# The first expert layer written without a loop over batches: weights loaded in order of need, two buffers of x, and the transposes, routing and normalisation of one batch placed inside its neighbours

## The chip, the cores and the metric

The kernel runs on one core of one Trainium2 chip. A core has a matmul engine (TensorE, PE in the rows, whose weight loads are listed apart as PEld), a vector engine (DVE), an activation engine (ACT), a general engine (GpSimd, POOL) and a synchronising engine (SP) that here only issues transfers; a row marked SPq or POOLq is a transfer being issued. The metric is the device time of one execution in microseconds; lower is better.

## The reference

Four layers run in sequence on x of shape (4, 512, 256): windowed attention, a mixture of experts, a gated delta rule, and a second mixture of experts, each followed by a residual sum and a layer norm. The change touches only the second of them:

```
B, S, D = x.shape                       # 4, 512, 256; E = 8 experts, K = 2
logits = xf @ gate_w
top_logits, top_idx = jax.lax.top_k(logits, K)
top_gates = jax.nn.softmax(top_logits, axis=-1)
gates = jnp.sum(jax.nn.one_hot(top_idx, E) * top_gates[..., None], axis=1)
h = gelu(jnp.einsum('nd,edh->neh', xf, w1) + b1)          # 256 -> 128 for each expert
out_e = jnp.einsum('neh,ehd->ned', h, w2) + b2            # 128 -> 256
routed = jnp.einsum('ne,ned->nd', gates, out_e)
shared = gelu(xf @ shared_w1 + shared_b1) @ shared_w2 + shared_b2   # 256 -> 256 -> 256
x = _layernorm(x + routed + shared)
```

All eight experts are computed for every token, and the gates weigh their outputs.

## The kernel before

The layers are functions that run one after the other, with a barrier of all engines between them; x passes from one to the next through a tensor in HBM (`mid_x` in the rows; each function reads one and writes another). `layer0_experts` (names with `f_`) works on a batch of 512 tokens at a time, four in all. It has ten hidden units of 128: units 0 and 1 are the shared expert, units 2 to 9 the eight experts.

On TensorE a batch goes through these steps. The tokens x are transposed, eight blocks of 128x128 (L705), into two PSUM banks `turn0` and `turn1`, and ACT copies them to `xT` (L752). Sixteen matmuls of 8 columns each make the routing logits (L710; a float32 matmul is two rows of the trace, a transpose one). `hide(n)` makes hidden unit n: four rows of 512 columns into one of two banks `hid` (L718), which ACT turns into `h` through gelu (L761), one of four buffers. The gates, made by DVE from the logits (L792 to L809, with one Exp on ACT, L754), are transposed in four rows (L738) and copied by ACT (L758). `project(u)` makes a sum: u = 0 is the shared expert's two units plus the biases weighted by the gates (16 rows of L728 and 8 of L731), every other u one expert (8 rows of L728), into one of two banks `sum`. DVE adds each sum into y, weighted by its gate (L815 for u = 0, with x; L818 for the others), then measures mean and variance (L823, L827, L829), POOL raises the variance to the power -0.5 (L772), DVE normalises (L833) and POOL issues the store (L775).

The order on each engine is the order of the code, and semaphores tie the engines: `hide(n)` waits for the gelu of unit n-2, `project(u)` for the gelu of its own unit and for the sum of u-2 to have been added. TensorE's order within a batch is hide 0, 1, 2, transpose of the gates, then hide(3+u) and project(u) in turns, which leaves project 7 and 8 (and, after hide 9, project 6) without a hide between them.

Every engine runs its part in a hardware loop over the four batches (`Fori`), and the whole of a batch is done before the next begins. At the start SP issues twelve loads (identity, gate weights, b2, w2, w1, b1) on one semaphore `loaded`, for which TensorE, ACT and DVE all wait in full, and then x of batch 0. There is one buffer of x: x of the next batch is issued when the last sum of the batch before has been added (`sp.wait_ge(added, F_SUMS * b)`, L694).

Of the kernel before, what the change touches and what calls it, by code (L numbers as in the profile page):

```python
# [18 lines left out]
ALU = mybir.AluOpType  # L19
# [615 lines left out]
def layer0_experts(nc, d):  # L635

    ctx, sems = ExitStack(), []
    with ctx:
# [14 lines left out]
        x, xT = sb("x", [P, NT, C]), sb("xT", [P, CK, T])  # L653
# [14 lines left out]
        loaded, x_in, x_turned, xT_ready, consts = sem("loaded"), sem("x_in"), sem("x_turned"), sem("xT_ready"), sem("consts")  # L668
# [5 lines left out]
        k_chain = 10  # L674

        carrier, carrier_pool = sem("carrier"), sem("carrier_pool")
        block = ctx.enter_context(nc.Block())

        @block.sync
        def _(sp):  # L680
            loads = [(ident[:], d["c_ident"]), (w_gate[:], d["L0_ffn_gate_w"].rearrange("(k p) n -> p k n", p=P)),
                     (b2[0:F_E, :], d["L0_ffn_b2"]), (b2[F_E:F_E + 1, :], d["L0_ffn_shared_b2"].rearrange("(a n) -> a n", a=1)),
                     (w2[:, 0:F_SH, :], d["L0_ffn_shared_w2"].rearrange("(k p) n -> p k n", p=P)),
                     (w2[:, F_SH:, :], d["L0_ffn_w2"].rearrange("e p n -> p e n"))]
            for k in range(CK):
                loads += [(w1[:, k, 0:F_SH, :], d["L0_ffn_shared_w1"][k * P:(k + 1) * P, :].rearrange("p (e n) -> p e n", e=F_SH)),
                          (w1[:, k, F_SH:, :], d["L0_ffn_w1"][:, k * P:(k + 1) * P, :].rearrange("e p n -> p e n"))]
            for dst, src in loads:
                sp.dma_start(dst, src).then_inc(loaded, 16)
            with nc.allow_non_contiguous_dma(reason="biases, one value a partition"):  # L690
                sp.dma_start(b1[:, 0:F_SH], d["L0_ffn_shared_b1"].rearrange("(e p) -> p e", p=P)).then_inc(loaded, 16)
                sp.dma_start(b1[:, F_SH:], d["L0_ffn_b1"].rearrange("e p -> p e")).then_inc(loaded, 16)
            with sp.Fori(0, BATCH) as b:
                sp.wait_ge(added, F_SUMS * b)  # L694
                sp.dma_start(x[:], x1_b[b, :, :, :]).then_inc(x_in, 16)

        @block.tensor
        def _(pe):
            pe.wait_ge(loaded, 16 * 12)
            with pe.Fori(0, BATCH) as b:  # L700
                pe.wait_ge(x_in, 16 * b + 16)
                pe.wait_ge(gT_ready, b)
                for k in range(CK):
                    for t in range(NT):
                        last = nc.tensor.transpose(TB[k][:, t * P:(t + 1) * P], x[:, t, k * P:(k + 1) * P], ident[:])  # L705
                last.then_inc(x_turned, 1)
                pe.wait_ge(xT_ready, 2 * b + 2)
                for t in range(NT):
                    for k in range(CK):
                        last = nc.tensor.matmul(TB[0][:, t * F_E:(t + 1) * F_E], xT[:, k, t * P:(t + 1) * P], w_gate[:, k, :],  # L710
                                                start=k == 0, stop=k == CK - 1)
                last.then_inc(routed, 1)

                def hide(n):

                    pe.wait_ge(gelued, F_UNITS * b + max(n - 1, 0))
                    for k in range(CK):
                        last = nc.tensor.matmul(HB[n % 2][:], w1[:, k, n, :], xT[:, k, :], start=k == 0, stop=k == CK - 1)  # L718
                    last.then_inc(hidden, 1)

                def project(u):

                    chunks = range(F_SH) if u == 0 else [u + F_SH - 1]
                    pe.wait_ge(gelued, F_UNITS * b + chunks[-1] + 1)
                    pe.wait_ge(added, F_SUMS * b + max(u - 1, 0))
                    for t in range(NT):
                        for n in chunks:
                            last = nc.tensor.matmul(YB[u % 2][:, t, :], h[:, n % 4, t * P:(t + 1) * P], w2[:, n, :],  # L728
                                                    start=n == chunks[0], stop=u > 0)
                        if u == 0:  # L730
                            last = nc.tensor.matmul(YB[0][:, t, :], gatesT[:, t * P:(t + 1) * P], b2[:], start=False, stop=True)  # L731
                    last.then_inc(summed, 1)

                for n in range(F_SH + 1):
                    hide(n)
                pe.wait_ge(gated, b + 1)
                for t in range(NT):
                    last = nc.tensor.transpose(TB[1][0:F_E + 1, t * P:(t + 1) * P], gates[:, t, :], ident[:])  # L738
                last.then_inc(g_turned, 1)
                pe.wait_ge(gT_ready, b + 1)  # L740
                for u in range(F_SUMS):
                    if F_SH + 1 + u < F_UNITS:
                        hide(F_SH + 1 + u)
                    project(u)

        @block.scalar
        def _(act):
            act.wait_ge(loaded, 16 * 12)
            with act.Fori(0, BATCH) as b:
                act.wait_ge(x_turned, b + 1)  # L750
                for k in range(CK):
                    nc.scalar.activation(xT[:, k, :], TB[k][:], ACT.Copy).then_inc(xT_ready, 1)  # L752
                act.wait_ge(shifted, b + 1)
                nc.scalar.activation(weight[:], weight[:], ACT.Exp).then_inc(exped, 1)  # L754
                for n in range(F_UNITS):
                    if n == F_SH + 1:
                        act.wait_ge(g_turned, b + 1)
                        nc.scalar.activation(gatesT[:], TB[1][0:F_E + 1, :], ACT.Copy).then_inc(gT_ready, 1)  # L758
                    act.wait_ge(hidden, F_UNITS * b + n + 1)
                    act.wait_ge(summed, F_SUMS * b + (0 if n < 4 else max(n - 4 - F_SH + 2, 1)))  # L760
                    nc.scalar.activation(h[:, n % 4, :], HB[n % 2][:], ACT.Gelu, bias=b1[:, n:n + 1]).then_inc(gelued, 1)  # L761

        @block.gpsimd
        def _(pool):
# [5 lines left out]
            with pool.Fori(0, BATCH) as b:  # L770
# [8 lines left out]
        def _(dve):  # L779
            dve.wait_ge(loaded, 16 * 12)  # L780
            dve.wait_ge(consts, 4)
            with dve.Fori(0, BATCH) as b:
                count = [0]

                def link(ins):

                    count[0] += 1
                    ins.then_inc(chain, 1)
                    dve.wait_ge(chain, k_chain * b + count[0])

                dve.wait_ge(routed, b + 1)
# [12 lines left out]
                link(nc.vector.tensor_tensor(mask[:], swapped[:, :, 0:F_E], logits[:, :, 0:F_E], ALU.not_equal))  # L804
                dve.wait_ge(exped, b + 1)
# [3 lines left out]
                nc.vector.tensor_tensor(gates[:, :, 0:F_E], weight[:], total[:, :, None].broadcast_to([P, NT, F_E]),  # L809
                                        ALU.mult).then_inc(gated, 1)  # L810
                dve.wait_ge(gated, b + 1)
                for u in range(F_SUMS):
# [1549 lines left out]
```

## Time and profile before

| | |
|---|---|
| time before, median of 3 runs | 2175.42 us |
| the three runs | 2175.3, 2175.42, 2187.16 us |
| the profiled execution: its own time | 2183.15 us |
| the profiled execution: its span (first to last instruction) | 2181.5 us |
| mean granted TensorE clock of the span | 0.878 |
| busy share PE / PEld / DVE / ACT / POOL | 78% / 50% / 48% / 30% / 32% |
| the stretch of `layer0_experts`, first load issued to last store issued | 599.93 to 833.73 us |

The profiled execution took 1.65 us more than its span and 7.7 us more than the median of the three runs. Of its 2181.5 us, the changed function has 234, or 11%. A clock of 1.00 in the rows is TensorE at 2.4 GHz, 0.50 at 1.2 GHz.

### The profile page before, as it was taken

What the parts mean: (1) busy time and instruction counts of PE and PEld (TensorE: products, weight loads), DVE (VectorE), ACT (ScalarE), POOL (GpSimd) and SP (SyncE); (2) the same over time, 40 slices, a digit from 0 to 9 for tenths busy, and PEclk for the clock granted to TensorE, in tenths of its full rate; (3) what the DMA queues carried; (4) which work ended last, traced back from release to release, by engine and by line L of the source; (5) the groups of instructions that cost most, each with busy time, mean ns of one, the idle gap of its engine ahead of it and who ended that gap; (6) DMA issues with size and microseconds to landing.
All of it is one profiled execution on the core that took longest, in us unless ns stands there. A gap on an engine that the chain in (4) does not pass through costs nothing. (4 is left out here: it accounts for less than half of the span.)

```text
span 2181.5 us, 29241 instructions
## 1 busy us (share of the span) xinstructions
PE 1692.8 (78%) x10666; PEld 1080.1 (50%) x10666; DVE 1050.4 (48%) x2394; ACT 659.2 (30%) x1159; POOL 692.0 (32%) x1099
## 2 busy tenths in 40 slices
PE   4887887988668885546699999999999964677771
PEld 3443444444345553222366666666666753444651
DVE  4746355462213332354556666776676521333623
ACT  2141431513212222323344444444544310111010
POOL 2010200200000000002767777787777631000142
PEclk8999898999879887867899999999999865888596
DMA  1000000000020002224112222212222213110074
GB/s 44 1 1 1 20 1 20 1 1 11 11 60 19 19 19 65 77 83 99 25 35 40 49 50 49 40 33 46 39 41 44 35 25 86 63 63 29 22 164 107
DMA packets 215799, 89.29 MB, mean 41 GB/s; under 512 B 166441, under 2 KB 208658, under 8 KB 215426
## 3 DMA queue, kind: packets, MB, share of 16 engines
q1 hardware_dynamic: 202658, 66.99, 13.9%
q0 software_dynamic: 6960, 18.88, 3.2%
q10 hardware_dynamic: 6064, 1.86, 0.4%
q8 instruction: 74, 1.21, 0.2%
q14 instruction: 43, 0.35, 0.1%
HBM read 53.39 MB, written 34.31 MB: 40 GB/s over the span
## 5 line engine op out<-in xcount | busy, mean ns | idle before, releaser
L1641 DVE SCALAR_TENSOR_TENSOR d_conv<-d_prep,d_cw,d_conv 128x511 f32<-128x511 f32 (+2 forms) x288 | 214.5, 746 | 39.7 <-ACT d_conv L1470 32.9
L1256 PE MATMUL d_prep<-d_hT,d_w 128*128 128x512 f32 x384 | 189.9, 619 | 27.1 <-DMA d_cw<-L_attn_conv_wq 18.3
L1592 POOL TENSOR_TENSOR d_prod<-d_blk 64x30 f32<-64x30 f32 (+4 forms) x360 | 174.3, 484 | 102.8 <-DMA d_blk<-mid_a_blk 75.6
L1596 POOL TENSOR_TENSOR d_blk<-d_blk,d_prod 64x30 f32<-64x30 f32 (+4 forms) x360 | 184.9, 514 | 28.2
L419 ACT ACTIVATE a_probs<-a_acc 128x896 f32<-128x896 f32 x128 | 117.5, 918 | 220.4 <-PE a_acc L244 132.0
L516 DVE TENSOR_REDUCE a_top<-a_turn 128x4 f32<-128x512 f32 (+3 forms) x240 | 147.3, 652 | 62.0 <-PE a_turn L207 54.0
L465 POOL TENSOR_TENSOR a_rstd<-a_rstd,a_mhalf 128x4 f32<-128x4 f32 x4 | 4.1, 1028 | 407.7 <-DVE a_rstd L565 407.7
L1256 PEld LDWEIGHTS d_prep<-d_hT,d_w 128*128 128x128 f32 x384 | 68.5, 198 | 88.4 <-issue 69.4
L1295 PE MATMUL d_prep<-d_kq 128*128 128x256 f32 x384 | 96.6, 396 | 15.3 <-DVE d_qkT L1673 15.3
L1470 ACT ACTIVATE d_conv<-d_prep,d_cw 128x512 f32<-128x512 f32 x96 | 66.1, 689 | 139.7 <-PE d_prep L1256 139.5
L1295 PEld LDWEIGHTS d_prep<-d_kq 128*128 128x128 f32 x384 | 73.6, 199 | 43.8 <-DVE d_qkT L1673 27.1
L206 PE MATMUL a_turn<-a_kS,a_qS 128*128 128x128 bf16 (+3 forms) x256 | 64.9, 306 | 32.6 <-DVE a_top L516 29.5
L718 PE MATMUL f_hid<-f_xT,f_w 128*128 128x512 f32 x160 | 82.6, 646 | 5.2 <-ACT f_gatesT L758 3.5
L728 PE MATMUL f_sum<-f_w,f_h 128*128 128x256 f32 x320 | 77.9, 384 | 0.1
L818 DVE SCALAR_TENSOR_TENSOR f_y<-f_sum,f_gates,f_y 128x256 f32<-128x256 f32 x128 | 53.1, 477 | 47.1 <-PE f_sum L728 46.6
L1583 POOL TENSOR_TENSOR d_mean<-d_mean,d_mhalf 128x16 f32<-128x16 f32 x12 | 38.9, 3241 | 108.5 <-DVE d_mean L1753 108.5
L772 POOL TENSOR_TENSOR f_rstd<-f_rstd,f_mhalf 128x4 f32<-128x4 f32 x4 | 4.1, 1030 | 217.9 <-DVE f_rstd L829 217.9
L451 POOL TENSOR_SCALAR a_stack<-a_parts 128x64 bf16<-128x64 bf16 x128 | 33.8, 297 | 120.6 <-DVE a_parts L501 120.6
L728 PEld LDWEIGHTS f_sum<-f_w,f_h 128*128 128x128 f32 x320 | 59.5, 190 | 25.1 <-issue 17.4
L1671 DVE SCALAR_TENSOR_TENSOR d_AT<-d_prep,d_a,d_decay 128x128 f32<-128x128 f32 x192 | 58.2, 346 | 22.3 <-PE d_prep L1295 21.9
L1445 ACT ACTIVATE d_kq<-d_conv 128x512 f32<-128x512 f32 x96 | 60.4, 629 | 24.4 <-DVE d_conv L1641 22.2
L1515 ACT ACTIVATE d_decay<-d_dec 128x512 f32<-128x512 f32 x48 | 28.7, 598 | 122.6 <-PE d_dec L1284 122.5
(353 smaller groups left out, 3728.7 us busy)
## 6 DMA issues: line engine op xcount, KB each, us to landing
mid_gate<-p_gate POOLq DMA_DIRECT2D x4, 768.0 KB, 4.0
mid_v<-p_v_tok POOLq DMA_DIRECT2D x3, 1024.0 KB, 6.0
d_v_h<-mid_v SPq DMA_DIRECT2D x12, 256.0 KB, 5.8
d_gate_h<-mid_gate SPq DMA_DIRECT2D x12, 256.0 KB, 5.5
mid_a_blk<-d_AT SPq DMA_DIRECT2D x48, 64.0 KB, 2.0
d_blk<-mid_a_blk SPq DMA_DIRECT2D x12, 256.0 KB, 3.6
mid_u_blk<-d_blk SPq DMA_DIRECT2D x12, 256.0 KB, 2.9
mid_l_blk<-d_blkT SPq DMA_DIRECT2D x12, 256.0 KB, 3.7
```

What stands on the lines that cost most here:

```text
L206: nc.tensor.matmul(acc, q[:, i * P:(i + 1) * P], k[:, 0:w], start=True, stop=False)
L419: nc.scalar.activation(probs[:, g % 2, h % 4, u, 0:896], AB[u][:].rearrange("p a t -> p (a t)")[:, 0:896], ACT.Exp, scale=A_SCALE).then_in ...
L516: nc.vector.tensor_reduce(dst, src, AX.X, ALU.max).then_inc(maxed, 1)
L718: last = nc.tensor.matmul(HB[n % 2][:], w1[:, k, n, :], xT[:, k, :], start=k == 0, stop=k == CK - 1)
L728: last = nc.tensor.matmul(YB[u % 2][:, t, :], h[:, n % 4, t * P:(t + 1) * P], w2[:, n, :], start=n == chunks[0], stop=u > 0)
L1256: last = nc.tensor.matmul(PB[f % 2][:], w[:, n % 2, i, k, :], hT[:, k, b * T:(b + 1) * T], start=k == 0, stop=k == CK - 1)
L1295: last = nc.tensor.matmul(PB[f % 2][:, 2 * c * P:2 * (c + 1) * P], kq[:, n % KQ_BUFS, 0, b, t0:t0 + P], kq[:, n % KQ_BUFS, :, b, t0:t0 + P ...
L1445: nc.scalar.activation(kq[:, n % KQ_BUFS, i, b, :], conv[:, f % 2, :], ACT.Silu).then_inc(silued, 1)
L1470: nc.scalar.activation(conv[:, f % 2, :], PB[f % 2][:], ACT.Copy, scale=cw[:, n % 2, f % 2, TAPS - 1:TAPS]).then_inc(scaled, 1)
L1592: nc.gpsimd.tensor_tensor(pr, blk[:, 0:t, t:t + 1].broadcast_to([lanes, t, m]), blk[:, t:t + 1, t + 1:BLK].broadcast_to([lanes, t, m]), AL ...
L1596: nc.gpsimd.tensor_tensor(blk[:, 0:t, t + 1:BLK], blk[:, 0:t, t + 1:BLK], pr, ALU.subtract).then_inc(subst, 1)
L1641: ins = nc.vector.scalar_tensor_tensor(dst, PB[f % 2][:, 0:T - j], cw[:, n % 2, f % 2, TAPS - 1 - j:TAPS - j], dst, ALU.mult, ALU.add)
```

## The change

The loops over batches become plain Python loops, so that each engine has the instructions of all four batches in a row and pieces of one batch can stand between those of another.

- Loads: identity, x of batch 0 and the gate weights come first; TensorE and ACT wait for identity and gate weights (`first_in`) and for x. Then the six transfers of w1 and b1 (`w1_in`, waited for before the first hide and, on ACT, before the first gelu), then b2 and w2 (`w2_in`, before the first project), then x of batch 1. x of batch 2 and 3 is issued when the first sum of batch b-2 has been added.
- Two buffers of x, xT, gates and y, by the parity of the batch.
- TensorE: batch b+1 is transposed after project 2 of batch b, routed after project 3, its gates transposed after project 7; hides 0 and 1 of batch b+1 take the place between project 6, 7 and 8 where batch b has no hide left.
- ACT: the copies of xT stand after gelu 5, the Exp after gelu 8, the copy of the gates after gelu 0 of the next batch.
- DVE: the routing of batch b+1 stands after the sums 3 (`choose`) and 5 (`weigh`), the normalisation of batch b-1 after sum 1 of batch b.

```diff
-        x, xT = sb("x", [P, NT, C]), sb("xT", [P, CK, T])
+        x, xT = sb("x", [P, 2, NT, C]), sb("xT", [P, 2, CK, T])
-        gates, gatesT = sb("gates", [P, NT, F_E + 1]), sb("gatesT", [F_E + 1, T])
+        gates, gatesT = sb("gates", [P, 2, NT, F_E + 1]), sb("gatesT", [F_E + 1, T])
-        y, x2 = sb("y", [P, NT, C]), sb("x2", [P, NT, C])
+        y, x2 = sb("y", [P, 2, NT, C]), sb("x2", [P, NT, C])
...
         @block.sync
...
-            for dst, src in loads:
-                sp.dma_start(dst, src).then_inc(loaded, 16)
...
-            with sp.Fori(0, BATCH) as b:
-                sp.wait_ge(added, F_SUMS * b)
-                sp.dma_start(x[:], x1_b[b, :, :, :]).then_inc(x_in, 16)
+            def load_x(b):
+                if b >= 2:
+                    sp.wait_ge(added, F_SUMS * (b - 2) + 1)
+                    sp.sem_inc(carrier_sp)
+                sp.dma_start(x[:, b % 2, :, :], x1_b[b, :, :, :]).then_inc(x_in[b % 2], 16)
+
+            sp.dma_start(ident[:], d["c_ident"]).then_inc(first_in, 16)
+            load_x(0)
...
+            for b in range(1, BATCH):
+                load_x(b)
...
         @block.tensor
-            pe.wait_ge(loaded, 16 * 12)
-            with pe.Fori(0, BATCH) as b:
+            pe.wait_ge(first_in, 32)
...
+            def hide(b, n):
+                unit = F_UNITS * b + n
+                if unit == 0:
+                    pe.wait_ge(w1_in, 16 * 6)
+                if unit >= 2:
+                    pe.wait_ge(gelued, unit - 1)
...
+            def project(b, u):
+                chunks = range(F_SH) if u == 0 else [u + F_SH - 1]
+                total_u = F_SUMS * b + u
+                if total_u == 0:
+                    pe.wait_ge(w2_in, 16 * 4)
+                if u == 0:
+                    pe.wait_ge(gT_ready, b + 1)
+                pe.wait_ge(gelued, F_UNITS * b + chunks[-1] + 1)
+                if total_u >= 2:
+                    pe.wait_ge(added, total_u - 1)
...
+            turn_x(0)
+            route(0)
+            hide(0, 0)
+            hide(0, 1)
+            for b in range(BATCH):
+                hide(b, F_SH)
+                if b == 0:
+                    turn_gates(0)
                 for u in range(F_SUMS):
                     if F_SH + 1 + u < F_UNITS:
-                        hide(F_SH + 1 + u)
-                    project(u)
+                        hide(b, F_SH + 1 + u)
+                    elif b + 1 < BATCH:
+                        hide(b + 1, F_SH + 1 + u - F_UNITS)
+                    project(b, u)
+                    if b + 1 < BATCH:
+                        if u == 2:
+                            turn_x(b + 1)
+                        if u == 3:
+                            route(b + 1)
+                        if u == 7:
+                            turn_gates(b + 1)
...
         @block.scalar
...
+            keep_x(0)
+            raise_gates(0)
+            act.wait_ge(w1_in, 16 * 6)
+            for b in range(BATCH):
                 for n in range(F_UNITS):
...
+                    if n == (1 if b else F_SH + 1):
+                        keep_gates(b)
+                    gelu(b, n)
+                    if b + 1 < BATCH:
+                        if n == 5:
+                            keep_x(b + 1)
+                        if n == 8:
+                            raise_gates(b + 1)
...
         @block.vector
...
+            choose(0)
+            weigh(0)
+            for b in range(BATCH):
+                for u in range(F_SUMS):
+                    add(b, u)
+                    if u == 1 and b:
+                        normalise(b - 1)
+                    if b + 1 < BATCH:
+                        if u == 3:
+                            choose(b + 1)
+                        if u == 5:
+                            weigh(b + 1)
+                measure(b)
+            normalise(BATCH - 1)
```

On TensorE, the end of one batch and the start of the next stand like this before: the last hide (`f_hid`, 512 columns) and the projects 6 to 8 (`f_sum`) close the loop's body,

```order
 L718 MATMUL f_hid<-f_xT,f_w 128x512 x2
 L725 REGISTER_ALU
 L728 MATMUL f_sum<-f_w,f_h 128x256 x4
 L724 REGISTER_ALU
 L725 REGISTER_ALU
 L728 MATMUL f_sum<-f_w,f_h 128x256 x4
 L724 REGISTER_ALU
 L725 REGISTER_ALU
 L728 MATMUL f_sum<-f_w,f_h 128x256 x4
 L700 REGISTER_ALU
 L700 COMPARE_AND_BRANCH
```

and the body begins again with the transposes of x (`f_turn` from `f_x`), the routing (`f_turn` from `f_xT`) and hides 0 and 1:

```order
 L700 ISA
 L705 MATMUL f_turn<-f_ident,f_x 128x128 x8
 L707 ISA
 L710 MATMUL f_turn<-f_w_gate,f_xT 128x8 x8
 L716 REGISTER_ALU
 L718 MATMUL f_hid<-f_xT,f_w 128x512 x4
```

In the changed kernel, on the same engine in the middle of batch 0 (hide 5, project 2 and on):

```order
 L741 MATMUL f_hid<-f_xT,f_w 128x512 x2
 L756 MATMUL f_sum<-f_w,f_h 128x256 x4
 L717 MATMUL f_turn<-f_ident,f_x 128x128 x8
 L741 MATMUL f_hid<-f_xT,f_w 128x512 x2
 L756 MATMUL f_sum<-f_w,f_h 128x256 x4
 L724 MATMUL f_turn<-f_w_gate,f_xT 128x8 x8
 L741 MATMUL f_hid<-f_xT,f_w 128x512 x2
 L756 MATMUL f_sum<-f_w,f_h 128x256 x4
```

The transposes and the routing of batch 1 have moved between hides and projects of batch 0. On ACT the piece around them is this now (gelus are `f_h`, the Exp of the routing `f_weight`):

```order
 L791 ACTIVATE f_xT<-f_turn 128x512 x2
 L806 ACTIVATE f_h<-f_hid,f_b 128x512 x3
 L795 ACT_TABLE_LOAD
 L795 ACTIVATE f_weight<-f_weight 128x32
 L806 ACT_TABLE_LOAD
 L806 ACTIVATE f_h<-f_hid,f_b 128x512 x2
 L799 ACTIVATE f_gatesT<-f_turn 9x512
```

where before both table loads stood ahead of a batch's first gelu:

```order
 L752 ACT_TABLE_LOAD
 L752 ACTIVATE f_xT<-f_turn 128x512 x2
 L754 ACTIVATE f_weight<-f_weight 128x32
 L759 ISA
 L760 REGISTER_ALU
 L761 ACT_TABLE_LOAD
 L761 ACTIVATE f_h<-f_hid,f_b 128x512
```

The pair of table loads has moved from the head of a batch to between gelu 8 and gelu 9 of the batch before. SP's queue is now, with x of batch 0 (L688) second where it stood thirteenth:

```order
 L690 DMA f_ident<-c_ident 128x128
 L688 DMA f_x<-mid_x 128x4x256
 L692 DMA f_w_gate<-L_ffn_gate_w 128x2x8
 L694 DMA f_w<-L_ffn_shared_w 128x256 x2
 L696 DMA f_b<-L_ffn_shared_b 128x2x1
 L697 DMA f_b<-L_ffn_b 128x8x1
 L699 DMA f_w<-L_ffn_w 128x8x128 x2
 L703 DMA f_b<-L_ffn_b 8x256
 L703 DMA f_b<-L_ffn_shared_b 1x256
 L703 DMA f_w<-L_ffn_shared_w 128x2x256
 L703 DMA f_w<-L_ffn_w 128x8x256
 L688 DMA f_x<-mid_x 128x4x256 x3
```

All of w1 and b1 stand ahead of b2 and w2, and x of batch 1 follows the weights without waiting for anything.

## Rows read from the trace of the kernel before

**Rows 1.** Stretch: length, busy PE PEld DVE ACT POOL, clock, DMA share, GB/s

```profile
668.74:722.99 54.25, 46.17 (x157) 29.30 (x157) 20.04 (x67) 11.14 (x16) 1.83 (x2) 0.88 0.06 19
```

**Rows 2.** Timeline at the stage's start: start, length, instruction [idle before, releaser]

```profile
600.33 0.43 SPq L689 DMA_DIRECT2D f_w_gate<-L_ffn_gate_w  x1
...
609.54 1.46 SPq L695 DMA_DIRECT2D f_x<-mid_x  x1
613.11 1.28 ACT L752 ACT_TABLE_LOAD   x1 [30.20 <-DMA f_b<-L_ffn_b]
...
614.34 1.97 PE L705 MATMUL f_turn<-f_ident,f_x 128*128 128x128 f32 x8 [26.01 <-DMA f_x<-mid_x]
```

**Rows 3.** Timeline from the last matmuls of batch 0 to batch 1's fourth hide

```profile
657.29 5.64 PE L728 MATMUL f_sum<-f_w,f_h 128*128 128x256 f32 x24
664.79 0.39 SPq L695 DMA_DIRECT2D f_x<-mid_x  x1
668.74 1.97 PE L705 MATMUL f_turn<-f_ident,f_x 128*128 128x128 f32 x8 [5.81 <-DMA f_x<-mid_x]
671.89 3.58 PE L710 MATMUL f_turn<-f_w_gate,f_xT 128*128 128x8 f32 x16 [1.18 <-ACT f_xT L752]
675.32 5.24 PE L718 MATMUL f_hid<-f_xT,f_w 128*128 128x512 f32 x8
682.81 0.60 PE L738 MATMUL f_turn<-f_ident,f_gates 128*9 128x128 f32 x4
684.30 1.98 PE L718 MATMUL f_hid<-f_xT,f_w 128*128 128x512 f32 x4 [0.89 <-ACT f_gatesT L758]
```

**Rows 4.** Timeline in the middle of batch 0, one hide and project

```profile
645.24 1.88 PE L718 MATMUL f_hid<-f_xT,f_w 128*128 128x512 f32 x4
646.96 1.89 PE L728 MATMUL f_sum<-f_w,f_h 128*128 128x256 f32 x8
647.24 0.69 ACT L761 ACTIVATE f_h<-f_hid,f_b 128x512 f32<-128x512 f32 x1 [2.83 <-PE f_hid L718]
648.68 1.88 PE L718 MATMUL f_hid<-f_xT,f_w 128*128 128x512 f32 x4
648.89 1.66 DVE L818 SCALAR_TENSOR_TENSOR f_y<-f_sum,f_gates,f_y 128x256 f32<-128x256 f32 x4 [1.78 <-PE f_sum L728]
```

**Rows 5.** Timeline, start of project 0 of batch 0 and the hide behind it

```profile
631.61 1.03 PE L728 MATMUL f_sum<-f_w,f_h 128*128 128x256 f32 x4
...
638.25 1.98 PE L718 MATMUL f_hid<-f_xT,f_w 128*128 128x512 f32 x4
```

**Rows 6.** Timeline, the transposes of batch 2

```profile
722.99 1.97 PE L705 MATMUL f_turn<-f_ident,f_x 128*128 128x128 f32 x8 [5.56 <-DMA f_x<-mid_x]
```

**Rows 7.** Transposes, matmuls of the next function: timeline

```profile
843.05 30.38 SPq L921 DMA_DIRECT2D p_x<-mid_x  x4
848.34 1.97 PE L943 MATMUL p_turn<-p_ident,p_x 128*128 128x128 f32 x8 [21.85 <-DMA p_x<-mid_x]
859.32 1.04 PE L943 MATMUL p_turn<-p_ident,p_x 128*128 128x128 f32 x8
```

**Rows 8.** Transfers in 604 to 606 us and 610 to 612 us

```profile
DMA packets 649, 0.66 MB, mean 332 GB/s; under 512 B 1, under 2 KB 649, under 8 KB 649
DMA packets 2031, 0.41 MB, mean 206 GB/s; under 512 B 1276, under 2 KB 2031, under 8 KB 2031
```

**Rows 9.** Timeline, the Exp of batch 0

```profile
622.28 0.23 ACT L754 ACTIVATE f_weight<-f_weight 128x32 f32<-128x32 f32 x1 [4.85 <-DVE f_weight L798]
```

**Rows 10.** Stretches as in rows 1: this stage, delta rule early, delta rule late

```profile
627.00:640.00 13.00, 12.11 (x40) 6.25 (x39) 1.23 (x1) 1.86 (x4) 0.00 (x0) 1.00 0.00 0
1200.00:1300.00 100.00, 94.45 (x659) 67.28 (x658) 66.52 (x147) 47.02 (x91) 70.55 (x104) 1.00 0.32 54
1740.00:1760.00 20.00, 18.45 (x106) 14.63 (x105) 6.03 (x17) 1.39 (x5) 17.57 (x32) 0.50 0.00 0
```

**Rows 11.** Timeline, one run of narrow matmuls in the last of these stretches

```profile
1749.16 1.92 PE L1394 MATMUL d_rec<-d_S,d_kq 128*128 128x32 f32 x8
```

More of the change, by code:

```diff
@@ L709, in _ @@
                     for k in range(CK):
-                        last = nc.tensor.matmul(TB[0][:, t * F_E:(t + 1) * F_E], xT[:, k, t * P:(t + 1) * P], w_gate[:, k, :],
+                        last = nc.tensor.matmul(TB[0][:, t * F_E:(t + 1) * F_E], xT[:, b % 2, k, t * P:(t + 1) * P], w_gate[:, k, :],
                                                 start=k == 0, stop=k == CK - 1)
                 last.then_inc(routed, 1)
[L714 to L732, printed above, removed]
@@ L734, in _, with turn_gates @@
-                for n in range(F_SH + 1):
-                    hide(n)
+            def turn_gates(b):
                 pe.wait_ge(gated, b + 1)
                 for t in range(NT):
-                    last = nc.tensor.transpose(TB[1][0:F_E + 1, t * P:(t + 1) * P], gates[:, t, :], ident[:])
+                    last = nc.tensor.transpose(TB[1][0:F_E + 1, t * P:(t + 1) * P], gates[:, b % 2, t, :], ident[:])
                 last.then_inc(g_turned, 1)
-                pe.wait_ge(gT_ready, b + 1)
+            def hide(b, n):
[4 more added lines that the diff above has]
+                    pe.wait_ge(gelued, unit - 1)
+                for k in range(CK):
+                    last = nc.tensor.matmul(HB[unit % 2][:], w1[:, k, n, :], xT[:, b % 2, k, :], start=k == 0, stop=k == CK - 1)
+                last.then_inc(hidden, 1)
@@ new lines, in project @@
+            def project(b, u):
[8 more added lines that the diff above has]
+                    pe.wait_ge(added, total_u - 1)
+                for t in range(NT):
+                    for n in chunks:
+                        last = nc.tensor.matmul(YB[total_u % 2][:, t, :], h[:, (F_UNITS * b + n) % 4, t * P:(t + 1) * P], w2[:, n, :],
+                                                start=n == chunks[0], stop=u > 0)
+                    if u == 0:
+                        last = nc.tensor.matmul(YB[total_u % 2][:, t, :], gatesT[:, t * P:(t + 1) * P], b2[:], start=False, stop=True)
+                last.then_inc(summed, 1)
@@ L753, in _, with keep_gates @@
                 act.wait_ge(shifted, b + 1)
                 nc.scalar.activation(weight[:], weight[:], ACT.Exp).then_inc(exped, 1)
-                for n in range(F_UNITS):
[L756 to L761, printed above, removed]
+            def keep_gates(b):
+                act.wait_ge(g_turned, b + 1)
+                nc.scalar.activation(gatesT[:], TB[1][0:F_E + 1, :], ACT.Copy).then_inc(gT_ready, 1)
@@ L779, in _, with link, choose @@
         def _(dve):
-            dve.wait_ge(loaded, 16 * 12)
             dve.wait_ge(consts, 4)
[L782 to L789, printed above, removed]
+            count = [0]
+            def link(ins):
+                count[0] += 1
+                ins.then_inc(chain, 1)
+                dve.wait_ge(chain, count[0])
+            def choose(b):
                 dve.wait_ge(routed, b + 1)
@@ L836, in _ @@
                 dve.wait_ge(ln_done, b + 1)
[L837 removed]
+            choose(0)
+            weigh(0)
+            for b in range(BATCH):
+                for u in range(F_SUMS):
[9 more added lines that the diff above has]
+            normalise(BATCH - 1)
     nc.clear_and_free_semaphores(sems)
```

85 lines of the change are left out of this document (52 added, 33 removed).

## The prediction

> **What bounds the kernel now.** The page's chain of waits doesn't reach back to this function (it names only lines of the last function), so I read the stretch directly: first the busy times of one batch, then the timeline through it, then the two places where TensorE stands still. From the transposes of batch 1 to those of batch 2 are 54.25 us, of which TensorE is busy 46.2, DVE 20.0, ACT 11.1, POOL 1.8 [rows 1, 3, 6]. Only TensorE is near full. In the middle of a batch it has no gap: hide starts follow each other at 645.24 and 648.68, so hide and project take 3.44 us, 1.72 each, while one gelu takes 0.69 and one sum on DVE 1.66 [rows 4]. So the stage is bound by TensorE, and what counts is what a batch takes beyond its matmuls at full clock. Two things are beyond: TensorE waits from 662.93 (657.29 + 5.64) to 668.74 for x, which was only issued at 664.79, and then the transposes, the routing and the first hides run one behind the other with waits between them, at half clock: eight rows of hides take 5.24 us there, where four from start to start take 1.72 in mid-batch [rows 3, 4]. The mean clock of the batch is 0.88 [rows 1]. At the stage's start TensorE waits until 614.34 for x, issued thirteenth at 609.54 [rows 2].
>
> **The boundary between batches.** I work it out in two ways.
>
> First by content. A batch in the changed kernel is, on TensorE: ten hides, 10 x 1.72 = 17.2; projects 1 to 8, 8 x 1.72 = 13.8; project 0, from 631.61 to 638.25, 6.6 [rows 4, 5]; eight transposes; sixteen rows of routing; four of the gates, 0.6 [rows 3]. The transposes took 1.97 at half clock; the same eight of the next function took 1.04 at full clock, with the drain of the last, about 0.9 from start to start [rows 3, 7]. The routing took 3.58 and no row shows it at full clock: it is 1.8 if it halves as the transposes do, 3.6 if it doesn't; I take 1.8, since its spacing (3.58/16 = 0.22) is that of the transposes at half clock (1.97/8 = 0.25, drain included). Sum 17.2 + 13.8 + 6.6 + 0.9 + 1.8 + 0.6 = 40.9, against 54.25: 13.3 less, 11.5 if the routing stays at 3.6.
>
> Then by what goes. The gap for x: 5.8 before batch 1, 5.6 before batch 2 [rows 3, 6]. From the transposes to the fourth hide: 684.30 - 668.74 = 15.6 becomes 0.9 + 1.8 + 3 x 1.72 + 0.6 = 8.5, so 7.1. The last three projects of a batch run without a hide and take 5.64 where 3 x 1.72 = 5.2 would do: 0.4 [rows 3]. Together 13.2. I take 13.3 a boundary. There are three: **40 us**. The order shown of TensorE has nothing else in it: the number of matmuls stays.
>
> What hides the moved work, and what it costs if the cover is gone:
> - x of the next batch. x of batch 1 stands right behind the weights, x of batch 2 and 3 is issued after the first sum of the batch before the one that runs, a whole batch ahead, and takes 3.7 to 4.0 us from issue to the transposes (664.79 to 668.74) [rows 3]. Cost nothing.
> - Copies of xT. ACT makes two, done about 1.2 us after the transposes (idle of 1.18 before the routing [rows 3]), and between transposes and routing now stand a hide and a project, 3.44, with gelu 6 behind the copies. Spare 2 us.
> - The routing on DVE. Logits to gates took from 675.3 to before 682.81, with the Exp in between [rows 3]. Now `choose` has from project 3 to gelu 8 and `weigh` until after project 7: more than two pairs, 7 us, and DVE is at 20 of now 41 us, a sum of 1.66 in every 3.44. Sums wait behind the routing for about 2 us once, but `project(u)` waits only for the sum of u-2. Cost nothing.
> - The two table loads on ACT now stand between gelu 8 and gelu 9. Load, Exp, load, gelu are 1.28 + 0.23 + 1.28 + 0.69 = 3.5 [rows 2, 9, 4]. Behind gelu 9 TensorE's hide 1 of the next batch waits, which starts three pairs and the gates' transposes after hide 8: 3 x 3.44 + 0.6 = 10.9. Gelu 8 is over 2.7 after hide 8 starts (647.24 - 645.24 + 0.69), and the second load comes after hide 9: 3.44 + 2.0 + 1.28 + 0.69 = 7.4. Spare 3.5 us. Cost nothing, and if the Exp came 5 us late, about 1.5 a boundary.
> - Normalisation and store of a batch (POOL 1.0, DVE 1.4) leave the boundary, where they cost nothing either. They remain behind the last batch, with the same tail as before.
>
> **The stage's start.** x goes from the thirteenth place to the second. It is issued at 600.33, in the place of the gate weights [rows 2]. Before, the transposes followed an issue of x by 3.95 (batch 1), 4.8 (batch 0, behind the weights) and 5.3 (next function, behind nine small loads: 843.05 to 848.34) [rows 2, 3, 7]. That is 604.3 to 605.6; I take 604.8, the middle row, for 614.34: 9.5 less. Then hide 0 would come 6.6 later (transposes, copies, routing at half clock as before, 668.74 to 675.32 [rows 3]), at 611.4, and must find w1 and b1. Ahead of them in the queue are identity and x; with the 1.3 MB of w1 that makes 1.9 MB, at 332 GB/s 5.7 us; the 1276 tiny packets of b1 slowed a stretch of 2 us to 206 GB/s, 0.8 us [rows 8]. From a start of the flow at about 603 that gives 609.5, before 611.4. The other end is that they land no earlier than the whole did before, when ACT saw all twelve at 613.11 [rows 2]: 1.7 lost. b2 and w2 are needed only after three hides and the gates, past 618, when all had landed at 613.11 even with x behind. So **9.5 us**, bounds 7.0 (605.6 and 613.1) to 10.0.
>
> **The sum.** 40 + 9.5 = 49.5. The profiled execution would take 2183.15 - 49.5 = 2133.7; it stands 7.7 above the median of the runs, and nothing in its trace says where, so I take the difference off the median: 2175.42 - 49.5 = **2126 us**. The known bounds are 3 x 11.5 + 7.0 = 41.5 and 3 x 13.6 + 10.0 = 51: 2124 to 2134.
>
> **A rule against a row.** The granted clock is 1.00 with TensorE 93% busy in this stage (627 to 640) and 94% busy early in the delta rule, but 0.50 with it busy 18.45 of 20 us in the late delta rule [rows 10], where the rows include eight matmuls of 32 columns at a time [rows 11]. So being busy has not kept the clock up everywhere, and the change puts its narrowest work, the routing of 8 columns, into the middle of full-clock hides. The Trainium skill (TensorE: Matmul & The Clock Gate, "HAM oscillation — how this bites in real kernels") gives as its abstract rule that idle gaps of TensorE are to be avoided. By that rule no clock would be lost here, since no gap is left; by the row a loss can't be excluded, and it is the first rival below.
>
> **Rivals.**
> (1) The narrow block takes the clock down once a batch. Then transposes, routing and gates cost their half-clock time, 3.3 us more, and the hides behind them run as in rows 3 (5.24 for eight where 3.44 would do, 1.8 more): 5.1 a boundary, 15 in all, 2141. For it: rows 10 and 11. Against: the gates' transposes, also narrow, stand inside 627 to 640 at 1.00, and a project and a hide now stand between transposes and routing.
> (2) The overlap is won only in part: a moved step arrives late at each boundary and TensorE, whose order is fixed, stands before it. If the piece at the boundary is as long as today's wait for x (5.7), 17 come back, with w1 late 1.7 more: 2145. For it: three engines now hand over within a running batch (TensorE to ACT to DVE to ACT to DVE to TensorE). Against: the spares of 2 to 7 us above.
> (3) The change doesn't do what it says: x or w1 still come last because the transfers share the engines instead of following the queue. Then the front gives 0 to 3 instead of 9.5, and the boundaries still 40: 2132 to 2136. Against: x was issued last and was last to land.
> (4) Slower than before: denser work is granted half the clock. All four batches at 0.50 are 4 x 2 x 40.9 = 327 us where full clock takes 164; the 163 more outweigh the 49.5 won: 2289. It decides from the point where 30% of the matmul time (49.5/164) runs at half clock. For it: the row at 0.50 with TensorE 92% busy. Against: the same stretch is of narrow matmuls, and with wide ones the delta rule held 1.00 over 100 us at 94% busy [rows 10].
>
> **How the numbers follow.** Forecast (2124 to 2134, with the scatter of runs) 0.65; (1) 0.10; (2) 0.09; (3) 0.08; (4) 0.03; the rest, 0.05, is a mishap not named that eats most of the gain. The three runs lie within 12 us of each other, so a median can stand some us above the sum. The range 2117 to 2143 holds the forecast, (3), most of (1). Within 1% of 2175.42 is within 21.8 us, about what a measurement of this kernel can tell from no change; 2153.7 is its lower edge. Forecast, (1), (2) and (3) all lie below it: faster 0.92. Same 0.05, slower 0.03.
>
> **What would show it.** In the changed kernel's timeline: the first transposes near 604.8, the first hide near 611.4 without a wait for w1; from then on no idle of TensorE over 0.5 us until the last project; batches 41 us apart (from project 0 to project 0); the routing in 1.8 us; granted clock 1.00 from some 10 us after the first matmul on; the last store issued near 784 instead of 833.73. Waits of the routing for f_xT, of the gates' transposes for DVE, or of a hide for gelu 9 would show (2). A clock under 0.95 between 620 and 770 would show (1) or (4). The prediction is wrong if the rest of the program moves: its code is the same, so any shift there above the scatter would be a cause that I have not seen.

## The result

The changed kernel takes 2128.89 us in the median of four runs (2124.86 to 2131.51), the kernel before 2177.81 in the median of four (2175.3 to 2187.16): a ratio of 0.9762, 95% interval 0.9739 to 0.9785. That is 48.9 us less by the medians; 49.5 was predicted, as 2126 us.

The profiled execution of the changed kernel took 2124.86 us. Its timeline at the stage's start (start, length, instruction), to be held against [rows 2]:

```profile
597.52 0.35 SPq L690 DMA_DIRECT2D f_ident<-c_ident  x1
597.92 0.43 SPq L688 DMA_DIRECT2D f_x<-mid_x  x1
...
601.98 1.97 PE L717 MATMUL f_turn<-f_ident,f_x 128*128 128x128 f32 x8 [16.03 <-DMA f_w_gate<-L_ffn_gate_w]
...
605.19 3.58 PE L724 MATMUL f_turn<-f_w_gate,f_xT 128*128 128x8 f32 x16 [1.24 <-ACT f_xT L791]
608.62 5.05 PE L741 MATMUL f_hid<-f_xT,f_w 128*128 128x512 f32 x8
...
618.05 1.03 PE L756 MATMUL f_sum<-f_w,f_h 128*128 128x256 f32 x4
```

The transposes begin 4.5 us after the first load is issued, where it was 14.4, and the first hide follows the routing without a wait for w1. The stage begins 2.4 us earlier in this execution than in the profiled one of before, although nothing ahead of it was changed; so below I give a stage's length, from its first load to the first load of the next function (`p_ident`): 238.5 us before (599.93 to 838.47), and here 186.1. The row at its end before, then the rows here:

```profile
838.47 0.35 SPq L918 DMA_DIRECT2D p_ident<-c_ident  x1
```

```profile
779.02 0.79 POOL L834 DMA_DIRECT2D mid_x<-f_x  x1 [2.01 <-DVE f_x L902]
783.59 0.35 SPq L1001 DMA_DIRECT2D p_ident<-c_ident  x1
```

The middle of batch 0, with batch 1's transposes and routing inside, answers to [rows 3, 4]:

```profile
631.67 1.04 PE L717 MATMUL f_turn<-f_ident,f_x 128*128 128x128 f32 x8
632.55 1.88 PE L741 MATMUL f_hid<-f_xT,f_w 128*128 128x512 f32 x4
634.27 1.89 PE L756 MATMUL f_sum<-f_w,f_h 128*128 128x256 f32 x8
635.99 1.85 PE L724 MATMUL f_turn<-f_w_gate,f_xT 128*128 128x8 f32 x16
637.70 1.96 PE L741 MATMUL f_hid<-f_xT,f_w 128*128 128x512 f32 x4
...
658.87 1.03 PE L756 MATMUL f_sum<-f_w,f_h 128*128 128x256 f32 x4
...
699.69 1.03 PE L756 MATMUL f_sum<-f_w,f_h 128*128 128x256 f32 x4
```

No row carries an idle time any more. The last two are project 0 of batches 1 and 2: 40.8 us apart. The stretches (as in rows 1: PE, PEld, DVE, ACT, POOL, clock, DMA) show the stage full and at 2.4 GHz, after a start at 1.2:

```profile
600.00:614.00 14.00, 10.45 (x32) 6.95 (x32) 2.44 (x20) 3.27 (x6) 0.00 (x0) 0.59 0.89 256
660.00:680.00 20.00, 20.00 (x84) 13.27 (x85) 8.59 (x27) 3.15 (x5) 1.53 (x2) 1.00 0.15 52
```

The whole list of TensorE's waits between 612 and 774 us is 0.6 us long:

```profile
PE f_hid L741 <- ACT f_h L806: 0.4, 1, 0.4
PE f_sum L756 <- DVE f_y L882: 0.2, 1, 0.2
```

Everything outside the stage took 1943.0 us in the profiled execution of before and 1936.8 here. Over all the kernels of this study, whose code outside the stage is the same, it lay between 1935.0 and 1943.4. That scatter is why a stage's length is the sharper measure for the small effects below; it isn't a gain of the change. A stage's length comes from one profiled execution, though, and the front of the stage varies too: in five executions whose code is the same until project 0 of batch 0, that project came 20.5, 21.0, 21.5, 21.5 and 21.6 us after the first load. In the shortest, the changed kernel's above, the first three hides took 7.3 us up to the gates' transposes, in the longest 8.3, because the granted clock rose from 0.50 to 1.00 later: between 2.4 and 3.4 us after the first hide began in the one, between 5.8 and 6.8 in the other. So a difference under 1 us between two stages says little.

### The profile page after: what moved, and what is told of

Same layout as the page of the kernel before. It is cut to its first block and busy times, and to the rows that moved or that the text cites. A ratio compares the mean times of both kernels' runs of the same rounds, so it can differ in the third digit from the quotient of the medians.

```text
span 2122.9 us, 29031 instructions
## 1 busy us (share of the span) xinstructions
PE 1669.3 (79%) x10666; PEld 1066.5 (50%) x10666; DVE 1051.6 (50%) x2394; ACT 658.1 (31%) x1158; POOL 691.6 (33%) x1099
## 3 DMA queue, kind: packets, MB, share of 16 engines
q1 hardware_dynamic: 202658, 66.99, 14.4%
q8 instruction: 78, 1.28, 0.3%
## 5 line engine op out<-in xcount | busy, mean ns | idle before, releaser
L741 PE MATMUL f_hid<-f_xT,f_w 128*128 128x512 f32 x160 | 76.8, 607 | 0.4 <-ACT f_h L806 0.4
L1657 POOL TENSOR_TENSOR d_g_upto<-d_upto,d_g 128x512 f32<-128x512 f32 x48 | 52.8, 1117 | 37.9 <-PE d_dec L1367 31.7
```

The source lines that it names most:

```text
L741: last = nc.tensor.matmul(HB[unit % 2][:], w1[:, k, n, :], xT[:, b % 2, k, :], start=k == 0, stop=k == CK - 1)
```

## The experiments

**One part alone: the loads.** The kernel before with x of batch 0 second and the weights behind it on semaphores of their own, as in the change:

```diff
-            for dst, src in loads:
-                sp.dma_start(dst, src).then_inc(loaded, 16)
+            sp.dma_start(ident[:], d["c_ident"]).then_inc(first_in, 16)
+            sp.dma_start(x[:], x1_b[0, :, :, :]).then_inc(x_in, 16)
...
-            with sp.Fori(0, BATCH) as b:
+            with sp.Fori(1, BATCH) as b:
```

Expected: 

> The loop over batches of the kernel before, with only the loads reordered: identity, x of batch 0 and gate weights first, then w1 and b1, then b2 and w2, each waited for where it is first used. One buffer of x, batches one after the other. My theory (the front gain is its own, from x being second in the queue): 9.5 to 11 us less than before, first transposes 4.5 us after the first load is issued instead of 14.4, batches still 54.4 us apart. Rival (w1 and w2 take the place of x as what is waited for, and the overlap is what hides them): 0 to 4 us less, with a wait for w1 or w2 in the first batch.

Measured: 0.9977 of before, interval 0.9961 to 0.9993, so 5.0 us less (1.5 to 8.5; here and below, a time saved is worked out from the ratio and 2178 us); stage 230.2 us, 8.3 less.

```profile
596.84 0.35 SPq L681 DMA_DIRECT2D f_ident<-c_ident  x1
...
601.68 1.94 PE L707 MATMUL f_turn<-f_ident,f_x 128*128 128x128 f32 x8 [16.44 <-DMA f_w_gate<-L_ffn_gate_w]
...
656.67 1.97 PE L707 MATMUL f_turn<-f_ident,f_x 128*128 128x128 f32 x8 [5.77 <-DMA f_x<-mid_x]
```

The first transposes come 4.8 us after the first load as in my theory, there is no wait for w1 or w2, and the wait for x at the boundary is still 5.8. The front gained 9.6 (14.4 to 4.8), and the four batches took 0.6, 0.4, 0.1 and 0.1 us longer than before, which leaves 8.3, under the 9.5 to 11 expected. The 0.6 is the clock at the start again: from the first hide to the gates' transposes batch 0 took 8.1 us here, 7.4 before. The rival, 0 to 4 with a wait for w1 or w2, is out by the stage and by the missing wait; by the ratio alone it would not be.

**The other part alone: the overlap.** The changed kernel with the old order of loads and

```diff
             pe.wait_ge(first_in, 32)
+            pe.wait_ge(w1_in, 16 * 6)
+            pe.wait_ge(w2_in, 16 * 4)
```

Expected: 

> The changed kernel with its loads in the old order: TensorE waits for all twelve loads and x before its first transpose, everything else as changed. My theory (the parts add up): 40 to 42 us less than before, batches 40.8 us apart from project 0 to project 0, first transposes 14.4 us after the first load. Rival (part of the boundary gain needs the early start, for instance because x of batch 1 then comes late): under 36 us less, with a wait before the transposes of batch 1.

Measured: 0.9811 (0.9791 to 0.9831), 41.2 us less; stage 197.4, 41.2 less.

```profile
598.44 0.35 SPq L698 DMA_DIRECT2D f_ident<-c_ident  x1
...
613.27 1.94 PE L718 MATMUL f_turn<-f_ident,f_x 128*128 128x128 f32 x8 [26.41 <-DMA f_x<-mid_x]
...
643.90 1.04 PE L718 MATMUL f_turn<-f_ident,f_x 128*128 128x128 f32 x8
```

The transposes of batch 1 carry no wait, and project 0 of batches 0 and 1 are 40.8 us apart, as in the changed kernel. The parts add up: 8.3 and 41.2 are 49.5 of the 52.5 that both give. Over half of the missing 3.0 is the start: from the first hide to the gates' transposes these two runs took 8.1 and 8.2 us, the changed kernel 7.3.

**Only the wait for x taken out.** The kernel before with

```diff
-            with sp.Fori(0, BATCH) as b:
-                sp.wait_ge(added, F_SUMS * b)
+            sp.dma_start(x[:], x1_b[0, :, :, :]).then_inc(x_in, 16)
+            with sp.Fori(1, BATCH) as b:
+                sp.wait_ge(added, F_SUMS * b - (F_SUMS - 1))
```

Expected: 

> The loop of the kernel before with one number changed: x of the next batch is issued when the first sum of the running batch has been added (its last reader), not the last; still one buffer, still one batch after the other. It takes the wait for x (5.6 us, three times) out of the boundary and leaves the chain transposes, copy, routing, hides. Theory A (the clock falls because of that wait): the clock stays at 1.00 through the chain, which gives back transposes 1.1, routing 1.8 and hides 1.8 as well: 17 + 14 = 31 us less than before. Theory B (the chain of short waits and narrow matmuls takes the clock down by itself): 17 us less, clock 0.50 in the chain. Then the overlap proper is worth 10 (A) or 24 (B) of the 41.

Measured: 0.9935 (0.9916 to 0.9954), 14.2 us less; stage 219.9, 18.6 less. The amount is that of theory B (17), not of A (31), but the clock did not do what B says at the first boundary. Timeline there:

```profile
659.54 1.04 PE L706 MATMUL f_turn<-f_ident,f_x 128*128 128x128 f32 x8
661.75 1.95 PE L711 MATMUL f_turn<-f_w_gate,f_xT 128*128 128x8 f32 x16 [1.17 <-ACT f_xT L753]
664.83 1.38 DVE L834 TENSOR_SCALAR f_x<-f_y,f_mean_var,f_rstd 128x256 f32<-128x256 f32 x4 [1.26 <-POOL f_rstd L773]
666.78 0.19 DVE L793 COPY f_logits<-f_turn 128x32 f32<-128x32 f32 x1 [0.58 <-DVE f_x L834]
668.04 0.23 ACT L755 ACTIVATE f_weight<-f_weight 128x32 f32<-128x32 f32 x1 [6.34 <-DVE f_weight L799]
670.33 1.98 PE L719 MATMUL f_hid<-f_xT,f_w 128*128 128x512 f32 x4 [3.09 <-ACT f_h L762]
```

The wait for x is gone and the clock is 1.00 here (1.04 and 1.95 for transposes and routing). But a wait that had been hidden under it comes up: the logits, ready at 663.7, are taken by DVE at 666.78, because the normalisation of the batch before, itself waiting for POOL, is ahead of them in DVE's order. Exp, table load and gelu come late by that much, and TensorE stands 3.1 us before hide 2. At the next boundary the clock then fell as well:

```profile
712.00:716.00 4.00, 2.29 (x6) 0.74 (x4) 3.19 (x21) 0.95 (x2) 0.79 (x1) 1.00 0.16 57
716.00:720.00 4.00, 2.68 (x3) 1.17 (x4) 0.58 (x4) 1.83 (x3) 0.00 (x0) 0.54 0.21 74
```

It fell at the third too (0.54 from 762 to 768 us). From transposes to project 0 the three boundaries took 15.9, 19.7 and 15.9 us, where they took 17.4, 17.5 and 17.5 before: what the clock gave back at two of them was mostly lost at the other. So the gain is, within a microsecond or two, the three waits for x themselves (17.2). Early loading alone is worth 18.6 of the 41.2, and the other 22.6 need the overlap, which moves the normalisation behind sum 1 and leaves TensorE no chain to wait through.

**Narrow work for the clock.** The changed kernel with

```diff
-                for t in range(NT):
+                for t in [t for _ in range(6 if b else 1) for t in range(NT)]:
```

in `route`. Expected: 

> The changed kernel with the routing matmuls of batches 1 to 3 run six times over (80 more rows of 8 columns a batch, same values). Tests the first rival of the prediction, that narrow work takes the clock down. If the clock holds at 1.00: 80 x 0.108 = 8.6 us a batch, 26 more than the changed kernel, so about 26 less than before. If a block of 10 us of narrow matmuls brings the clock to 0.50 while it runs and for some us behind it: 19 us and more a batch, 58 to 63 more than the changed kernel, so 8 to 12 more than before; half of that if it falls halfway through.

Measured: 0.9994 of before (0.9978 to 1.001), so 48 to 49 us more than the changed kernel by the medians; stage 236.9, 50.8 more. That is neither of the two amounts expected (26, or 58 to 63), but the clock fell in each block. (A routing is eight matmuls of 8 columns, sixteen rows of the trace; six of them are 96 rows.) Timeline and stretches of batch 1's block:

```profile
637.61 15.87 PE L724 MATMUL f_turn<-f_w_gate,f_xT 128*128 128x8 f32 x96
653.33 3.44 PE L741 MATMUL f_hid<-f_xT,f_w 128*128 128x512 f32 x4
...
640.00:642.00 2.00, 2.00 (x21) 2.00 (x20) 0.00 (x0) 0.00 (x0) 0.00 (x0) 1.00 0.00 0
644.00:646.00 2.00, 2.00 (x11) 2.00 (x10) 0.00 (x0) 0.00 (x0) 0.00 (x0) 0.50 0.00 0
```

TensorE is busy 2.00 of 2.00 us in both, as the profile counts it, and the clock falls from 1.00 to 0.50 all the same; the hide behind the block takes 3.44 instead of 1.88. Blocks of 15.9, 17.4 and 17.3 us for 1.85 make 45 us, three slow hides 5: the 50.8. The mechanism of the first rival is real; but the block that the change itself makes, 16 rows between hides, ran at 1.00 throughout.

**How much the routing chain has to spare.** The changed kernel, with twelve copies on ACT before the Exp, and in a second run with five:

```diff
+                for i in range(12 if b else 0):
+                    nc.scalar.activation(idle[:, i, :, :], x[:, b % 2, 0:2, :], ACT.Copy)
                 act.wait_ge(shifted, b + 1)
```

Expected for twelve: 

> The changed kernel with twelve copies of 512 columns on ACT (0.6 us each, 7.2 us) between gelu 8 and the Exp of the next batch's routing. My theory (gelu 9 has 3.5 to 4.5 us to spare): TensorE waits 3 to 4 us a boundary, 9 to 12 more than the changed kernel. Rival (the routing chain, Exp to gates to their transposes, is what is tightest): the same delay shows as a wait of the gates' transposes instead, and more, since 7.2 us reach project 7: 15 or more.

Expected for five: 

> The changed kernel with five copies on ACT (0.53 us each, 2.6 us) between gelu 8 and the Exp of the next batch's routing, where twelve (6.3 us) cost 2 us a boundary. If what is to spare there is the 3.5 to 4.5 us that the prediction worked out: no wait on TensorE, the stage 186 to 187 us as changed. If the spare is less than 2 us and the twelve were paid for elsewhere: 1 us a boundary and more.

Measured: twelve 0.9802 (0.9787 to 0.9817), five 0.9746 (0.9713 to 0.9778). Twelve copies took 6.3 us together, not 7.2, and the stage 192.3: 6 us more than the mean of the changed kernel's two (186.1, and 186.6 in the run below), 5.3 of them in the three periods, which were 42.6 us from project 0 to project 0 and not 40.8. Five copies took 2.7 us and left the period at 40.8; their stage, 187.0, is 0.7 more within the scatter of its start. TensorE's waits from batch 0 on, of twelve, and the first two in its timeline:

```profile
PE f_turn L732 <- DVE f_gates L872: 2.6, 3, 0.9
PE f_hid L742 <- ACT f_h L809: 1.3, 3, 0.4
```

```profile
654.62 0.60 PE L732 MATMUL f_turn<-f_ident,f_gates 128*9 128x128 f32 x4 [0.88 <-DVE f_gates L872]
655.66 1.98 PE L742 MATMUL f_hid<-f_xT,f_w 128*128 128x512 f32 x4 [0.44 <-ACT f_h L809]
```

With five there is none of either. The list of waits seems to say that the gates' transposes are tightest, as the rival has it, since they are met first and carry 2.6 of the 3.9 us. The starts say otherwise. With the Exp 6.2 us later against the hides, the gates' transposes came 1.05 us late, so 5.2 were to spare there, and hide 1 of the next batch, which waits for gelu 9, came 1.65 late in all, so gelu 9 had 4.6. The same 4.6 can be read in the changed kernel, where gelu 9 ends at 647.37 (its row, 646.68, is shown at the end of this document) and hide 1 begins at

```profile
651.99 1.88 PE L741 MATMUL f_hid<-f_xT,f_w 128*128 128x512 f32 x4
```

So gelu 9 sets the price, as in my theory, and its wait looks small only because the gates' stands in front of it. The amounts expected, 9 to 12 and 15 or more, were both too high: the copies were shorter than assumed, and the 1.8 us a boundary are the 1.65 by which hide 1 was late and 0.1 in the row behind it.

**The bias matmuls.** The changed kernel with `b2` and `gatesT` as tiles of 128 rows, zero below row 8:

```diff
-        b1, b2 = sb("b1", [P, F_UNITS]), sb("b2", [F_E + 1, C])
+        b1, b2 = sb("b1", [P, F_UNITS]), sb("b2", [P, C])
...
-        gates, gatesT = sb("gates", [P, 2, NT, F_E + 1]), sb("gatesT", [F_E + 1, T])
+        gates, gatesT = sb("gates", [P, 2, NT, F_E + 1]), sb("gatesT", [P, T])
...
+            nc.gpsimd.memset(b2[:], 0.0).then_inc(consts, 1)
+            nc.gpsimd.memset(gatesT[:], 0.0).then_inc(consts, 1)
```

Beside it, on the same chip, the changed kernel again. Expected of that: 

> The changed kernel once more, as the measure for the three below on the same chip: 0.976 of before, the stage from its first load to the next function's first load 186 us.

Expected of the wider bias: 

> The changed kernel with the bias matmuls of project 0 widened from 9 to 128 rows of contraction: b2 and the transposed gates are filled with zeros below row 8. Project 0 takes 6.64 us for 24 rows of 256 columns, 0.28 each, where the other projects take 0.215 a row. Theory A (the 9-row weights, next to 128-row ones, are what slows them): project 0 goes to 24 x 0.215 = 5.2 us, 1.5 a batch, 6 us less than the changed kernel. Theory B (the cost is the change between two sources, or the accumulation): no change.

Measured: the changed kernel 0.9772 (0.9755 to 0.9789), stage 186.6; the wider bias 0.9734 (0.9721 to 0.9748), stage 179.8, 6.5 less than the mean of the two stages as changed, of which the four projects 0 make 5.8. Project 0 and the hide behind it, to be held against [rows 5]:

```profile
618.72 1.03 PE L758 MATMUL f_sum<-f_w,f_h 128*128 128x256 f32 x4
619.59 0.59 PE L761 MATMUL f_sum<-f_b,f_gatesT 128*128 128x256 f32 x2
...
623.90 1.88 PE L743 MATMUL f_hid<-f_xT,f_w 128*128 128x512 f32 x4
```

5.2 us instead of 6.6: theory A. Multiplying 119 rows of zeros cost no time, and the matmuls that contract over 9 rows, among those over 128, did. Theory B is out, since the alternation of the two sources and the accumulation are the same in both. Why the 9 rows cost time stays open.

**The clock at the start.** The changed kernel with a tile `warm` of ones, filled by POOL, and two matmuls on it before TensorE's first wait:

```diff
+            nc.gpsimd.memset(warm[:], 1.0).then_inc(warm_in, 1)
...
+            pe.wait_ge(warm_in, 1)
+            for _ in range(2):
+                nc.tensor.matmul(HB[0][:], warm[:, 0:P], warm[:], start=True, stop=True)
             pe.wait_ge(first_in, 32)
```

Expected: 

> The changed kernel with two matmuls of 512 columns on a tile of ones before x has landed, while TensorE otherwise waits; their result is overwritten. Theory A (the clock rises with work before the first transposes): batch 0's transposes, routing and first hides run partly at 1.00, 2 to 5 us less than the changed kernel. Theory B (it needs the same stretch of work whenever that begins, and the waits in the chain break it): no change, or up to 1 us more if the two matmuls are still running when x lands.

and the same with the wider bias and one more such matmul behind `turn_x(0)`. Expected: 

> The changed kernel with the 128-row bias matmuls of the run before, the two matmuls on ones ahead of x, and a third between the transposes of batch 0 and its routing, in the 1.2 us in which TensorE waits for the copy of xT. In the run with two of them the clock was at 1.00 for the transposes and fell to 0.50 in the routing, whose sixteen rows took 3.46 us. Theory A (the pause before the routing let it fall): the clock stays up, the routing takes 1.9 us, the hides follow once w1 has landed, and the stage is 2 to 4 us shorter than with the 128-row bias matmuls alone (179.8 us). Theory B (the narrow rows of the routing themselves take it down): 0 to 1 us shorter, the routing again 3.4 us.

Measured: two alone 0.9769 (0.9753 to 0.9784), stage 185.5, 0.9 less than the mean of the changed kernel's two; with bias and the third 0.971 (0.9684 to 0.9737), stage 179.5, 0.3 less than the wider bias alone, which is within the scatter. The start of the first, then of the second:

```profile
596.87 3.42 PE L713 MATMUL f_hid<-f_warm 128*128 128x512 f32 x4 [12.16 <-POOL f_warm L829]
600.70 1.10 PE L722 MATMUL f_turn<-f_ident,f_x 128*128 128x128 f32 x8 [0.41 <-DMA f_w_gate<-L_ffn_gate_w]
603.04 3.46 PE L729 MATMUL f_turn<-f_w_gate,f_xT 128*128 128x8 f32 x16 [1.24 <-ACT f_xT L796]
```

```profile
603.73 1.02 PE L770 MATMUL f_hid<-f_warm 128*128 128x512 f32 x2
605.15 1.95 PE L731 MATMUL f_turn<-f_w_gate,f_xT 128*128 128x8 f32 x16 [0.40 <-ACT f_xT L800]
608.74 5.29 PE L748 MATMUL f_hid<-f_xT,f_w 128*128 128x512 f32 x8 [1.64 <-DMA f_w<-L_ffn_w]
```

Of the first, theory A holds for the transposes (1.10 us instead of 1.97) and not for the rest: the clock was down again in the routing. Its 0.9 us is under the 2 to 5 expected and within the scatter of the stage's start, so whether two matmuls alone win anything is not shown. Of the second, theory A on the clock holds: with the pause filled it stayed up, and the routing took 1.95 instead of 3.46. Its amount, 2 to 4 us, does not: the hides wait 1.6 us for w1 instead, the clock is down behind that, and they take 5.29 as before. The start now waits for the load where it had waited for the routing. Whether the 1.6 us of waiting or the narrow rows before them took the clock down, this run can't tell apart. Of the two that beat the changed kernel the one with both is lowest, but its interval and that of the wider bias alone overlap.

## Why the prediction was right

**The boundary.** Predicted 54.25 to 40.9, taken as 13.3 three times, 40. Measured from project 0 to project 0: 40.8, against 54.5 before, so 13.7 three times, 41.1; and 41.2 with this part alone. The content of TensorE was the right measure because nothing else came up. The routing at full clock, for which there was no row, took 1.85; 1.8 was chosen over 3.6.

**The start.** The transposes were predicted 4.9 us after the first load is issued, measured 4.5; hide 0 at 11.5, measured 11.1. By the trace it was the gate weights, third in the queue, that ended TensorE's wait, and not x: x landed 3.8 us after its issue at 597.92, the gate weights 3.5 after theirs at 598.40, some 0.2 later. The transposes don't read the gate weights; they share the semaphore `first_in` with the identity. w1 was in time, but by less than worked out: predicted 9.6 us after the first load (609.5), 1.9 before hide 0. The last run, in which hide 0 could have begun 1.6 us earlier and waited for w1, shows it at 10.5, which is 0.6 before hide 0 of the changed kernel. In all 9.5 predicted, 9.95 measured until the transposes (14.41 to 4.46).

**The sum.** 49.5 predicted; the stage gave 52.5. The 3.0 more are 0.5 of x, 1.1 of the boundaries, 0.2 at the end, and 1.2 that I had left out: in batch 0 the fourth hide no longer waits for the gates' copy (0.9 [rows 3]), since only project 0 waits for it now; with it the way from transposes to project 0 shrinks from 17.3 to 16.1. The last of these is in part the clock's rise at the start: in the other four executions with the same start that way took 16.5 to 17.1. With the changed kernel run again the stage gave 52.0. So by the stage the sum was 2.5 to 3 us too low. The medians moved by 48.9, less than the stage, within the scatter of the rest of the program; that they came within 0.6 of 49.5 is in part luck.

**The covers.** Spare was given as 3.5 us for gelu 9, 2 for the copies of xT, and more for the gates, without a figure. The run with twelve copies puts gelu 9 at 4.6 and the chain from the Exp to the gates' transposes at 5.2; the copies of xT ended at 633.84 and the routing began at 635.99, 2.15 later. So gelu 9 was the tighter of the two, as predicted, with a microsecond more than worked out.

**The rivals.** The first, the clock, was right in its mechanism and wrong in its size: it took the clock down in blocks of 96 narrow rows, and not in the 16 that the change moves. What was held against it, the gates' transposes at 1.00, was no evidence: by their rows (128*9, 128x128) only their weights are 9 wide, and each streams 128 columns, the routing 8. On the Trainium skill's rule on idle gaps (TensorE: Matmul & The Clock Gate, "HAM oscillation — how this bites in real kernels"): the changed kernel agrees with it, at 1.00 with no gap over 0.2 us from 614.07 us to its last project, and the run with six routings shows that having no gap is not enough. The second, a late hand-over, didn't occur in the changed kernel, but did in the run with x loaded early only: there DVE's order made TensorE wait 3.1 us. The third, loads that share the engines: x, second in the queue, landed some 4.2 us after the first load was issued, w1 only 6 us later. The fourth, half clock throughout: 1.00.

## What to carry to other kernels

Where one engine bounds a stage that is cut into batches, add up that engine's instructions at their full rate; the difference from the measured period is what an overlap can return, and it was returned here within 3%. Taking out only the wait that the trace names gave that wait back and hardly more: behind the wait for x stood another, for a normalisation in DVE's order, which the first had covered, and it took what the clock would have given. After such a change look at what has only a little to spare (w1, 0.6 us; gelu 9, 4.6), for that is what the next change will meet, and measure the spare from starts, since the list of waits can show the first of two late steps larger than the one that sets the price, as it did with the twelve copies.

## What the runs showed of the hardware

- TensorE's clock fell from 2.4 to 1.2 GHz while the profile counted the engine busy 2.00 of 2.00 us, in a block of 96 rows of 8 columns; in the changed kernel, with rows of 256 and 512 columns and busy 20.00 of 20.00, it stayed at 2.4.
- Two trace rows that contract over 9 partitions after every four that contract over 128 made project 0, 24 rows in all, take 6.6 us; with all at 128 it took 5.2.
- A table load of ACT in the middle of gelus costs its 1.28 us and nothing visible besides. In the changed kernel load, Exp, load and gelu stand with gaps of some 0.01 us:

```profile
643.85 1.28 ACT L795 ACT_TABLE_LOAD   x1
645.14 0.23 ACT L795 ACTIVATE f_weight<-f_weight 128x32 f32<-128x32 f32 x1
645.39 1.28 ACT L806 ACT_TABLE_LOAD   x1
646.68 0.69 ACT L806 ACTIVATE f_h<-f_hid,f_b 128x512 f32<-128x512 f32 x1
```
